# A four-layer graph network on one core: block positions in two levels, a wider first projection, a first pass that finishes per block, and the last layer as one stage

## The reference

```python
x = _layernorm(x + _L0_gnn_ref(x, edge_index, edge_attr_13, ...))    # attention, 4 heads, with edge features
x = _layernorm(x + _L1_gnn_ref(x, edge_weight1, ..., edge_type_64))  # relations, 8 bases
x = _layernorm(x + _L2_gnn_ref(x, edge_index, ...))                  # transformer, two convolutions
x = _layernorm(x + _L3_gnn_ref(x, edge_index, W1, b1, W2, b2))       # gcn, two convolutions
```

## Time and profile before

| | us |
|---|---|
| median of 3 runs | 4654.02 (4648.46 to 4659.68) |
| the profiled execution, its own time | 4652.1 |
| its span, first to last instruction | 4650.3 |
| VectorE busy in the span | 3001.2 (65%) |
| GpSimd busy | 2727.2 (59%) |
| TensorE busy, matmul | 2810.4 (60%) |
| ScalarE busy | 934.8 (20%) |

### The profile page before, as it was taken

One profiled execution on the slowest core, in us unless ns is written; L12 is line 12 of the kernel. 1 busy time (PEld: TensorE's weight loads), 2 busy tenths in 40 slices (PEclk: granted clock), 3 DMA queues, 4 the chain that ended last, 5 costly groups with the idle time before them and its releaser, 6 DMA issues. The chain is left out here.

```text
span 4650.3 us, 56109 instructions
## 1 busy us (share of the span) xinstructions
PE 2810.4 (60%) x18074; PEld 2599.7 (56%) x18075; DVE 3001.2 (65%) x6284; ACT 934.8 (20%) x781; POOL 2727.2 (59%) x2656
## 2 busy tenths in 40 slices
PE   1356656656614555556566456666666667994955
PEld 0356656656613555555556356655665657983744
DVE  6355655655676666676665477777777778996144
ACT  0121221211201222222221121221221123441000
POOL 0577777777705777777773277777777723551000
PEclk9566656656656677776668767777777779996977
DMA  1444444444404455445443356556655625540532
GB/s 20 109 98 110 102 99 109 100 102 109 98 21 103 134 135 136 136 132 136 135 133 90 84 138 154 147 146 153 153 144 149 153 56 123 115 106 1 171 95 92
DMA packets 169458, 526.18 MB, mean 113 GB/s; under 512 B 60851, under 2 KB 87800, under 8 KB 156470
## 3 DMA queue, kind: packets, MB, share of 16 engines
q1 hardware_dynamic: 74032, 299.78, 26.1%
q0 software_dynamic: 95264, 224.28, 18.6%
HBM read 456.40 MB, written 67.48 MB: 113 GB/s over the span
## 5 line engine op out<-in xcount | busy, mean ns | idle before, releaser
L544 POOL DMA_INDIRECT e0G<-table,e0src x858 | 851.9, 993 | 439.1 <-issue 405.1
L544 POOL DMA_INDIRECT e21G<-table,e21src x858 | 856.1, 998 | 408.1 <-issue 257.6
L1364 POOL DMA_INDIRECT t1G<-table,t1idx x806 | 789.7, 980 | 375.5 <-issue 242.0
L1437 PE MATMUL t1psW<-t1CO,t1G 128*128 128x192 f32 x1612 | 435.9, 434 | 303.9 <-issue 285.6
L1437 PEld LDWEIGHTS t1psW<-t1CO,t1G 128*128 128x128 f32 x1612 | 370.4, 258 | 312.2 <-issue 292.2
L568 PE MATMUL e21psQ<-Q,e21OT 121*128 x1716 | 412.5, 410 | 129.6 <-DVE e21G L682 54.3
L568 PEld LDWEIGHTS e21psQ<-Q,e21OT 121*128 121x128 f32 x1716 | 399.8, 326 | 141.4 <-issue 81.6
L561 PE MATMUL e0psQ<-Q,e0OT 121*128 x1716 | 398.7, 371 | 94.3 <-ACT e0OT L599 58.2
L561 PEld LDWEIGHTS e0psQ<-Q,e0OT 121*128 121x128 f32 x1716 | 396.6, 325 | 99.8 <-issue 99.8
L2103 POOL TENSOR_TENSOR e22Z<-e22Z,e22C 121x847 f32<-121x847 f32 (+1 forms) x104 | 200.1, 1955 | 259.0 <-ACT e22Z L2095 259.0
L584 PE MATMUL e21psA<-e21G,e21O 128*121 128x145 f32 x1716 | 272.4, 330 | 106.1 <-DVE e21G L733 106.1
(11 more groups left out here) (428 smaller groups left out, 5250.8 us busy)
## 6 DMA issues: line engine op xcount, KB each, us to landing
e0dstb<-in_dst_p SPq DMA_DIRECT2D x27, 1996.5 KB
e21dstb<-in_dst_p SPq DMA_DIRECT2D x27, 1996.5 KB
e22C<-counts SPq DMA_DIRECT2D x26, 1487.0 KB
Q<-in_type_p SPq DMA_DIRECT2D x62, 416.0 KB
counts<-X SPq DMA_DIRECT2D x13, 1487.0 KB
planes<-SKIP SPq DMA_DIRECT2D x26, 743.5 KB
counts<-RES SPq DMA_DIRECT2D x13, 1487.0 KB
e31C<-planes SPq DMA_DIRECT2D x26, 743.5 KB
```

Source lines behind the costliest of these rows:

```text
L544: nc.gpsimd.indirect_dma_start(out=G[:, u, t, 0:width], out_offset=None, in_=table, in_offset=bass.IndirectOffsetOnAxis(ap=src[:, u, t:t + ...
L1364: nc.gpsimd.indirect_dma_start(out=G[:, q % 2, t, :], out_offset=None, in_=table, in_offset=bass.IndirectOffsetOnAxis(ap=idx[:, q * GT + t ...
L1437: mmi = nc.tensor.matmul(psW[:, k % 2, 0:WIN * NBAS], G[:, q % 2, t, :], CO[:, k % 2, i].rearrange("p b w -> p (b w)"), start=(i == 0), st ...
```

## The change

`plan_and_project` takes the place of `plan_steps` and of p0: 27 partitions compare the first target of each of 806 tiles with the block's first node, GpSimd gathers for each block the one tile of 128 targets in which it begins, and two more operations count inside it. The projection runs in the same stage with a weight of 140 columns, of which 136 differ (the attention products are folded into the weight), and the table is stored in four parts; the load of x comes last among the loads. In `attention_pass` src of the first two steps is loaded ahead of all else, and in the loop SP loads the edges of step s + 1 first and src of step s + 2 behind them. For layer 0 `finish_block` finishes a block behind each step and ScalarE stores its rows into the table of 128 columns, so f0 and p1 fall away. `last_layer` keeps p31 and puts both sums in one stage: between the sums of two blocks TensorE turns and projects a finished block, VectorE splits it into bf16 parts, and in the second sum VectorE normalises two blocks at a time and SP stores them.

The diff, cut to its core (blank lines and most drains left out; the chain from `cum` to `ready` is that of `plan_steps`, word for word):

```diff
...
-        plan_steps(nc, a, X, eye, iota, pidx, base_t, off_t, neg_t, keep_t, steps_i)
+        plan_and_project(nc, a, X, Q, SKIP, eye, iota, pidx, base_t, off_t, neg_t, keep_t, steps_i, tab[132])
...
-        project(g, "p0", [("L0_gnn_W", None)], tab[132], "gat")
         attention_pass(g, "e0", tab[132], 132, 4, True)
-        gat_finish(g)
-        project(g, "p1", [], tab[128], "copy")
         relation_tiles(g, "t1", tab[128], tab[256])
...
-            for c in (1, 2):
-                project(g, f"p3{c}", [(f"L3_gnn_W{c}", None)], tab[128], "gcn", source=X if c == 1 else RES)
-                dense_sum(g, f"e3{c}")
-                gcn_finish(g, f"f3{c}", f"L3_gnn_b{c}", out if c == 2 else None)
+            project(g, "p31", [("L3_gnn_W1", None)], tab[128], "gcn")
+            last_layer(g, out)
...
         @block.sync
         def _(sp):
+            for u in range(2):
+                e = sp.value_load(g["steps_i"][0:1, SMAX + u:SMAX + u + 1], min_val=0, max_val=E)
+                load_edges(sp, a, src[:, u, :], "src_p", e, sources_in[u])
+                for i, n in enumerate(("L0_gnn_bias", "L0_gnn_ln_gamma", "L0_gnn_ln_beta")):
+                    sp.dma_start(aff[:, i, :], a[n].partition_broadcast(BN)).then_inc(S["consts"], 16)
...
             with sp.Fori(0, g["n_pairs"](sp)) as i:
                 for u in range(2):
                     s = i * 2 + u
-                    e = sp.value_load(g["steps_i"][0:1, bass.ds(s + SMAX, 1)], min_val=0, max_val=E)
+                    e = sp.value_load(g["steps_i"][0:1, bass.ds(s + (SMAX + 2), 1)], min_val=0, max_val=E)
                     e2 = sp.value_load(g["steps_i"][0:1, bass.ds(s + (SMAX + 1), 1)], min_val=0, max_val=E)
-                    sp.wait_ge(S["scores_made"], s + 1)
-                    sp.sem_inc(S["waited"], 1)
-                    load_edges(sp, a, src[:, u, :], "src_p", e, sources_in[u])
                     sp.wait_ge(S["edges_used"], s + 1)
                     sp.wait_ge(S["targets_ready"], s + 1)
                     sp.sem_inc(S["waited"], 1)
                     for buf, what in bufs:
                         load_edges(sp, a, buf[:] if what != "attr_p" else buf, what, e2, S["edges_in"])
+                    sp.wait_ge(S["scores_made"], s + 1)
+                    sp.sem_inc(S["waited"], 1)
+                    load_edges(sp, a, src[:, u, :], "src_p", e, sources_in[u])
...
+                    if gat:
+                        act.wait_ge(S["exp_wanted"], s + 1)
+                        nc.scalar.activation(fe[:], fs[:, 0:8], ACT.Exp).then_inc(S["exp_made"], 1)
+                        for k, x in enumerate((fc, fv, fv)):
+                            act.wait_ge(S["root_wanted"], s * 3 + (k + 1))
+                            nc.scalar.activation(x[:], x[:], ACT.Sqrt).then_inc(S["rooted"], 1)
+                        blk = act.value_load(g["steps_i"][0:1, bass.ds(s, 1)], min_val=0, max_val=NB - 1)
+                        act.wait_ge(S["row_ready"], s + 1)
+                        act.wait_ge(row_stored[1 - u], i * 16 + (16 + 16 * u))
+                        act.sem_inc(S["act_waited"], 1)
+                        act.dma_start(g["rows_table"].rearrange("(b p) f -> b p f", p=BN)[bass.ds(blk, 1)].rearrange("a p f -> (a p) f"),
+                                      xo[:, u, :]).then_inc(row_stored[u], 16)
...
+            def norm(x, s, count):
...
+                V.tensor_reduce(fm[:], x, AX.X, ALU.add)
+                V.tensor_scalar(fm[:], fm[:], 1.0 / D, None, ALU.mult)
+                V.tensor_scalar(x, x, fm[:], None, ALU.subtract)
+                V.tensor_tensor(ft[:], x, x, ALU.mult)
+                V.tensor_reduce(fv[:], ft[:], AX.X, ALU.add)
+                V.tensor_scalar(fv[:], fv[:], 1.0 / D, EPS, ALU.mult, ALU.add).then_inc(S["root_wanted"], 1)
+                dve.wait_ge(S["rooted"], s * 3 + count)
+                V.reciprocal(fv[:], fv[:])
+            def finish_block(s, i, u, blk):
...
+                V.tensor_copy(g["deg"][:, bass.ds(blk, 1)], cnt)
+                V.tensor_scalar(fc[:], cnt, 1.0, None, ALU.add).then_inc(S["root_wanted"], 1)
+                V.tensor_scalar(fm[:], cnt, 1.0, None, ALU.max)
+                V.reciprocal(fm[:], fm[:])
+                V.tensor_tensor(al, q(Q, 0, 4), q(Q, 4, 8), ALU.add)
+                V.scalar_tensor_tensor(out=al, in0=ST[:, plain:plain + 4], scalar=fm[:], in1=al, op0=ALU.mult, op1=ALU.add)
+                V.scalar_tensor_tensor(out=al, in0=al, scalar=0.2, in1=al, op0=ALU.mult, op1=ALU.max)
+                V.tensor_tensor(m, ST[:, D + H:D + 2 * H], al, ALU.max)
+                V.tensor_tensor(fs[:, 0:4], ST[:, D + H:D + 2 * H], m, ALU.subtract)
+                V.tensor_tensor(fs[:, 4:8], al, m, ALU.subtract).then_inc(S["exp_wanted"], 1)
+                dve.wait_ge(S["rooted"], s * 3 + 1)
+                V.reciprocal(g["cnt1"][:, bass.ds(blk, 1)], fc[:])
+                dve.wait_ge(S["exp_made"], s + 1)
+                V.tensor_tensor(den, ST[:, D:D + H], fe[:, 0:4], ALU.mult)
+                V.tensor_tensor(den, den, fe[:, 4:8], ALU.add)
+                V.tensor_scalar(den, den, 1e-16, None, ALU.add)
+                V.reciprocal(den, den)
+                V.tensor_tensor(fe[:].rearrange("p (k h) -> p k h", k=2), fe[:].rearrange("p (k h) -> p k h", k=2),
+                                bc(den.unsqueeze(1), [BN, 2, H]), ALU.mult)
+                hc = lambda x: x.rearrange("p (h c) -> p h c", h=H)
+                V.tensor_tensor(hc(fy[:]), hc(ST[:, 0:D]), bc(fe[:, 0:4].unsqueeze(2), [BN, H, C]), ALU.mult)
+                V.tensor_tensor(hc(ft[:]), hc(q(g["SKIP"], 0, D)), bc(fe[:, 4:8].unsqueeze(2), [BN, H, C]), ALU.mult)
+                V.tensor_tensor(fy[:], fy[:], ft[:], ALU.add)
+                V.tensor_tensor(fy[:], fy[:], aff[:, 0, :], ALU.add)
+                V.tensor_tensor(fy[:], fy[:], q(g["X"], 0, D), ALU.add)
+                norm(fy[:], s, 2)
+                V.scalar_tensor_tensor(out=fy[:], in0=fy[:], scalar=fv[:], in1=aff[:, 1, :], op0=ALU.mult, op1=ALU.mult)
+                V.tensor_tensor(fy[:], fy[:], aff[:, 2, :], ALU.add)
+                V.scalar_tensor_tensor(out=fy[:], in0=fy[:], scalar=0.0, in1=q(g["X"], 0, D), op0=ALU.max, op1=ALU.add)
+                norm(fy[:], s, 3)
+                dve.wait_ge(row_stored[u], i * 16 + 16)
+                V.tensor_scalar(xo[:, u, :], fy[:], fv[:], None, ALU.mult).then_inc(S["row_ready"], 1)
             V = nc.vector
...
-            dve.sem_inc(S["scores_made"], 2)
+            for u in range(2 if gat else 0):
+                dve.sem_inc(row_stored[u], 16)
...
+                    if gat:
+                        finish_block(s, i, u, blk)
+                    else:
+                        V.tensor_copy(RES[:, bass.ds(blk, 1), 0:NC].rearrange("p a f -> p (a f)"), ST[:])
...
+def last_layer(g, out):
...
+            def sums(b, parts, made):
+                for h in range(NB):
...
+            def turn(b, k):
+                pe.wait_ge(S["row_ready"], k * NB + (b + 1))
+                pe.wait_ge(S["row_copied"], k * NB + (b + 1))
+                nc.tensor.transpose(psT[:, b % 2, 0:BN], y[:, b % 2, :], eye[0:BN, 0:BN]).then_inc(S["row_turned"], 1)
+            def make(b, k):
+                pe.wait_ge(S["row_copied"], k * NB + (b + 3))
+                pe.wait_ge(S["row_taken"], k * NB + (b + 1))
+                nc.tensor.matmul(psY[0:BN, b % 2, 0:D], hT[:, b % 2, :], w2[:], start=True, stop=True).then_inc(S["row_made"], 1)
...
+            with pe.Fori(0, n) as k:
+                for b in range(NB + 2):
+                    if b < NB:
+                        pe.wait_ge(counts_in[b % RING], k * 32 + (b // RING * 16 + 16))
+                        pe.wait_ge(S["taken"], k * NB + (b + 1))
...
+                        sums(b, HP, S["summed"])
...
+                    if 1 <= b <= NB:
+                        turn(b - 1, k)
+                    if b >= 2:
+                        make(b - 2, k)
+            with pe.Fori(0, n) as k:
+                for b in range(NB):
...
+                    pe.wait_ge(S["taken2"], k * NB + (b + 1))
+                    if b == 0:
+                        pe.wait_ge(S["parts_ready"], n * NGRP)
...
+                    sums(b, HP2, S["summed2"])
...
+            def take(b, made, count, taken, acc):
+                dve.wait_ge(made, count)
+                V.tensor_reduce(part[:, b % 2], ps[0:BN, b % 2, 0:3 * D].rearrange("p (k f) -> p f k", k=3), AX.X, ALU.add).then_inc(taken, 1)
+                V.tensor_tensor(acc, acc, part[:, b % 2], ALU.add)
+            def row(b, k):
+                dve.wait_ge(S["row_made"], k * NB + (b + 3))
+                V.tensor_scalar(RES[:, b, 0:D], psY[0:BN, b % 2, 0:D], cnt1[:, b:b + 1], None, ALU.mult).then_inc(S["row_taken"], 1)
+                if b % GRP == GRP - 1 or b == NB - 1:
...
+                    V.tensor_copy(hp[:, :, 2, :], r).then_inc(S["parts_ready"], 1)
...
```

(80 more changed lines are left out.)

325 lines of the change are left out of this document (321 added, 4 removed).

## The result

The changed kernel takes 4446.5 us (median of 4 runs, 4443.3 to 4448.5) against 4653.1 (4 runs, 4648.5 to 4659.7): a ratio of 0.9554, 95% interval 0.9538 to 0.9571. The prediction was 4395 in a range of 4345 to 4480. The direction was right and the time lies in the range, but 52 us of the gain that was forecast didn't come. The profiled execution has a span of 4446.7, so the stages can be set beside the terms. Each stage is taken from its first transfer to that of the next, so e21's row holds the short finish behind it too (3787 to 3799 in the kernel before).

What follows compares the result with a forecast made beforehand. The prediction took e0 to be bound by GpSimd's gathers, with VectorE idle 13.7 us a step. Terms -78.7 - 17.1 + 5 + 16.2 - 94.1 - 13.4 - 76 = -258 gave 4395 us, range 4345 to 4480.

Steps and rivals of the forecast that it cites:

- A, the opening: Plan and projection before e0: a shorter search, x last, no separate products; e0 begins at 52.5 in place of 131.22, -78.7.
- B, the first gather: Start of e0: with sources loaded first, the first gather comes 3.4 us after the stage in place of 20.4, -17.1.
- C, the period: e0's steps: the 13.4 us finish fills VectorE's idle 13.7, period 43.8 becomes 44.0, +5; bounds -28 and +92.
- the first rival: e0: a heavier finish makes VectorE's turn 47 to 53 us, time 4470 to 4620; chance 0.09.
- The second rival: e0: GpSimd's gathers stand still while VectorE finishes a block, period 56.1, time 4697, slower than before; chance 0.04.
- The drain of 1.38 us: e0's finish: a drain beside each table load, left out of the sum; on the path it would add 35, about 4430.
- D and E, e0's end: After e0's last step: last finish and row store add 16.2; f0 and p1 falling away saves 94.1.
- F, e21: Start of e21: first gather 3.4 us after the stage in place of 16.8, -13.4, the gain going to the end.
- G, the last layer: Both sums in one stage with turns, products and normalisation between: -76, bounds -88 and -56.
- the third rival: Last layer: TensorE gets the half clock because it waits between blocks, 179 us more, time 4574; chance 0.04.
- the search in A: Opening: the two-level search's wide compare, sum and eight small operations, taken at 3.3 us.
- C's bound for a finish of 17: e0's period: the slow bound of its term, a finish of 17 us, given as +92.

Runs made afterwards that it cites:

- x_behind: Changed kernel with the load of x issued behind the landing of the 27 target tiles that the block search gathers: 4441 us.
- e0_written_out: Changed kernel with VectorE's loop of e0 written out as 26 steps with constant numbers, other engines keeping their loops: 4489 us.
- pad_before: Kernel before with 74 drains more at the head of each step of VectorE's loop in e0, 398 instructions in place of 250: 4662 us.
- best_pairs: Changed kernel with x loaded behind the tiles, no TensorE wait for its own sums, and e0's blocks finished two at a time: 4358.6 us, ratio 0.9376.
- old_sources: Changed kernel with the sources loaded as in the kernel before, behind the first edges and ahead of the next step's edges: 4486 us.

## Why the prediction came out as it did

**A, the opening**: -75.2 against -78.7. The step that failed here is the tile gather, taken at 3.0 from a load that had the queues to itself. It stood behind x's 1573 KB and took 8.3; in x_behind it takes 2.5, so 5.8 of it were the neighbour, and e0 begins 5.3 earlier. The start, the chain, the projection and the last store (49.1 to 56.0) came within 1.5 us each of their estimates.

**B, the first gather**: 2.7 us after the stage, 3.4 forecast. But step 0 is scored 54.3 us after the stage's first transfer, 12.6 less than before and not 17.1 less: the last of 33 gathers now ends at 104.3 and is awaited until 110.3, where it was 196.4 and 198.1. The edges of step 1 are asked for at 91 to 92.6 and are moving then, and the gathers of 95 to 111 take a median of 8.6 us from issue to landing, against 2.6 in the stage. That the edges are the reason is argued, not shown.

**C, the period**: the largest miss, and the step that failed. 44.0 was forecast, 45.5 came, 25 x 1.5 = 37 us. The size of the finish was right (13.6 against 13.4), and so was the turn of a step within the loop's body (43.9). What the sum lacked is what the longer loop costs at its turn, 3.4 us in every second step. The trace of before couldn't price it: its loop of 250 instructions is kept there (5 packets), and VectorE stood idle for 13.7 us a step in any case. e0_written_out took exactly this away; pad_before brought the fetching into a kernel that has no finish; best_pairs, with the finish in a loop of 343, is without it. It isn't a heavier finish, the first rival. That the time stays in the range is luck to this degree: C's upper bound was set for a heavier finish, and it was wide enough for a cost that the prediction doesn't name. The second rival, GpSimd standing still, is out: gathers beside the finish keep 0.94, and VectorE, not the gathers, is what the stage waits for. The drain of 1.38 us that the Trainium skill (ScalarE: Activation LUTs, What ACT_TABLE_LOAD costs) puts beside a table load doesn't show on the path here: the whole wait behind load and root is 1.88, of which the load is 1.28 and the root 0.20.

**D and E, e0's end**: from the last score to t1's first transfer 45.5 in place of 29.7 + 95.1, so -79.3 against 16.2 - 94.1 = -77.9.

**F, e21**: -15.1 against -13.4, and old_sources gives it back (15.4).

**G, the last layer**: -61.3 against -76. The mechanism was right, the term of waits was mis-sized: 0.3 us a block in the second loop and 0.2 in the first, where the wait for its own sum alone costs 0.56. The second loop took 126.4 where 117.3 were forecast, the first 134.6 where 131.4 were. Without that wait they take 111.7 and 120.2. Another 2.9 us lie ahead of the loops: the first sum began 11.0 after the stage's first transfer, where 8.1 were forecast. The tail was 8.4 against 9.5, and the granted clock was 1.00 and 0.99 in the loops (from 4176.6 and from 4311.6 on), so the third rival is out.

Some of the prediction's own additions are off by little: the search in A comes to 3.6 and not 3.3 (it took 2.9), B to 17.0, C's bound for a finish of 17 to +95 and not +92, and G's tail to 9.4. None of them bears on the account above.

## What to carry to other kernels

An edit that lengthens a loop's body can change the cost of its turn too: count the body's instructions before and after, and look at what hides the jump. Work that is put into an engine's waiting time uses up the cover of every small cost on that engine, the old ones and those that the work brings along; price the period with no cover at all. And a wait of an engine for its own last result, kept only to raise a counter, can be given to the engine that reads that result, as it was here.

## What the runs showed of the hardware

A loop on VectorE was either kept (3 to 5 instruction packets of 8 KB in a whole stage) or fetched anew in each of its 13 turns (65 to 67). Loops of 250 and of 343 instructions were kept at the one place each where they stood, those of 396 and 398 at none. The loop of 268 was kept in all runs but e0_written_out, where it was fetched although unchanged, and 64 more instructions ahead of it ended that. The price went from 3.4 us a turn in the changed kernel's e0 to 77 us in 13 turns, 6 each, in e21 of e0_written_out, where the gap grew to 13 us, part of it in place of waits for gathers, and GpSimd was held up. Why it differs stays open, and so do the exact length and the rule of place.
